# A two-layer image tower on one core: token search in three parts, chosen experts in the same stage, and a reordered first attention

## Chip, cores and metric

One core of one Trainium2 chip runs the whole program. The metric is the device time in microseconds (us) of that core. Of the kernel before, three runs are shown: 2080.99, 2083.64 and 2084.97, median 2083.64 us.

## What is computed

64 images of 3x224x224 are cut into 196 patches each, so there are 12544 tokens of width 128. Two layers follow:

```python
h = L0_tok(x)                                  # patches @ w + b
h = h + L0_attn(layernorm(h))                  # quantized q, k, v; causal attention inside one image
h = h + L0_ffn(layernorm(h))                   # each of 8 experts picks its own 1024 tokens
h = h + L1_attn(layernorm(h))                  # 8 heads
h = h + L1_ffn(layernorm(h))                   # each token picks 2 of 8 experts
# inside L0_ffn
logits = x_flat @ Wr                           # [12544, 8]
probs = softmax(logits, axis=0)                # over the tokens
vals, idx = top_k(probs.T, 1024)               # [8, 1024]
h = gelu(x_flat[idx] @ W1 + b1);  out_e = h @ W2 + b2
output = zeros.at[idx].add(vals[..., None] * out_e)
```

All 1024 tokens of an expert have to be found exactly, ties by the lowest token number. The change touches the first attention and the first expert layer (`L0_attn`, `L0_ffn`).

## The kernel before

The program has four stages, one behind the other, each with its own instruction streams for the five engines and with semaphores between them: `embed_and_attend`, `topk_experts`, `attend_and_route`, `routed_experts`. Between stages all engines meet.

**First attention, `embed_and_attend`.** The work is cut into 32 units of two images (4 tiles of 98 tokens). The engines run one software pipeline: in iteration n an engine does, for instance, the patch matmuls of unit n, the first norm and quantization of unit n-1, scores of unit n-2, mixing and projection of unit n-3 and the routing logits of unit n-4. The order inside an iteration is written out by hand for each engine, and an engine runs it strictly in order.

- SP (`emit_sp`, L380): in iteration n it first loads the images of unit n (12 DMAs, L270 and L271) once the pixels of unit n-2 have been copied out of the same half of the two-deep `img`, then it waits for the second norm of unit n-5 (L391) and stores `xn2` and `h2`, then the logits of unit n-6. The 12 loads of the next unit stand behind that wait in the queue.
- PE (L421): turn `hT` (L427), patches 0 and 1, turn `xd`, patch 2, the query-key matmul, turn `xn2` (L449), patch 3, turn `probs`, scores, patch 4, mix, patch 5, projection, patches 6 and 7, logits.
- ACT (L523): copies of `hcur`, `xdT`, `uT`; one copy of four pixel columns into `pix` (L539); `xn2T`, `probsT`, `mixT`; four exponentials (L559); `hT` with the bias (L566); the logits.
- DVE (L580): first norm and quantization of unit n-1 (L587 to L605), two row maxima for each image of unit n-2 (L614), and for unit n-3 the residual `h2`, its statistics and, after a wait for POOL's root (L636), the second norm `xn2` (L641).
- POOL (L647): the root for the first norm of unit n-1, two pixel columns (L664), the root for the second norm of unit n-3, two more pixel columns.

**Choice of tokens, first inner block of `topk_experts`.** The 8x12544 logits are read back as [128, 784]: 16 partitions for each expert. After maximum and exponential, a bisection (`settle`, L851) fixes the 30 bits of each expert's threshold probability from the top, one bit for each of 30 steps: DVE counts the values at or above a candidate (L854), PE sums the counts of the 16 partitions (L801), DVE updates `cur` and `bit`. Then prefix counts are formed (two scans, L874 and L881), written to DRAM (L751), read back twice with one row for each block of 112 tokens (L755, L756), and turned into a table `rise`. For each expert `past` marks the blocks that each of 1024 slots lies behind (L893), PE looks up the right block row by a matmul (L818), and DVE counts inside the block (L899). In all 16 groups of 512 slots are looked up, and then two instructions write all token numbers (L903, L904). POOL makes the constants of later stages meanwhile (`made.make`, `groups.constants`, L781).

**Chosen experts, second inner block (L940).** 16 groups of 512 tokens, two for each expert. POOL gathers the rows of a group with four indirect DMAs (L965) into a two-deep `xg`, PE turns them, computes the logit again for the weight, and the two layers (L1013, L998), ACT does the GELU (L1056) and the weighting (L1072), DVE adds the bias (L1112), and POOL adds the rows to `h` in DRAM with four indirect DMAs (L977). In its stream a gather of group n-1 and a scatter of group n-5 alternate. Before the scatter of every new expert POOL waits until the earlier scatters have landed (L972 to L974), since experts can share a token.

Of the kernel before, what the change touches and what calls it, by code (L numbers as in the profile page):

```python
# [15 lines left out]
D = 128  # L16
# [181 lines left out]
def embed_and_attend(nc, sb, ps, sem, early, x, w_tok, b_tok, wq, wk, wv, wr, hd_dram, ident, ident_b, ones,  # L198
                     mask_qk, halfpow, logits_dram, xn_dram):
    with ExitStack() as ph:  # L200
# [178 lines left out]
        def emit_sp(sp):  # L379
            def emit(n, k):  # L380

                if live(n, 0, UNITS) and not (isinstance(n, int) and n == 0):
                    wait(sp, pix_ready, n - 1, apart=True)
                    wait(sp, pix_ready_pool, 2 * (n - 1))
                    load_images(sp, n, k)
# [17 lines left out]
        def emit_pe(pe):  # L403
            def patch(n, k, js):
                if not live(n, 0, UNITS):
                    return
                if 0 in js:
                    wait(pe, pix_ready, n + 1)
                    wait(pe, hT_ready, n)
                if half // 2 in js:  # L410
                    wait(pe, pix_ready_pool, 2 * n + 2)
# [9 lines left out]
            def emit(n, k):  # L421
# [17 lines left out]
                if live(n, 2, UNITS):  # L439
# [4 lines left out]
                              start=True, stop=True).then_inc(u_ready, 1)  # L444
                if live(n, 4, UNITS):
# [5 lines left out]
                patch(n, k, [3])  # L451
# [70 lines left out]
        def emit_act(act):  # L522
            def emit(ahead, k_ahead):  # L523
# [6 lines left out]
                if live(n, 2, UNITS):  # L530
                    u = n - 2
                    wait(act, xd_turned, u + 1)
                    act.copy(xdT[:, (k - 2) % 2, :], p_tr[:, 0:COLS]).then_inc(xdT_ready, 1)
                    wait(act, u_ready, u + 1)
# [5 lines left out]
                if live(n, 4, UNITS):  # L540
                    u = n - 4
                    wait(act, xn2_turned, u + 1)
                    act.copy(xn2T[:, (k - 4) % 2, :], p_tr[:, 0:COLS]).then_inc(xn2T_ready, 1)
                if live(n, 3, UNITS):
                    u = n - 3
                    wait(act, probs_turned, u + 1)
                    for m in range(2):
                        act.copy(probsT[:, (k - 3) % 2, m, :], p_ptr[m][:, 0:CAUSAL]).then_inc(probsT_ready, 1)
                    wait(act, mixed, u + 1)
                    act.copy(mixT[:, (k - 3) % 2, :], p_mm[:, 0:COLS]).then_inc(mixT_ready, 1)  # L550
                if live(n, 2, UNITS):
                    u = n - 2
                    wait(act, max_ready, (u + 1) * 2)
                    if not isinstance(u, int) or u >= 4:
                        wait(act, h2_step, (u - 3) * H2_STEPS)
                    for m in range(2):
                        for i in range(2):
                            c = slice(0, TILE) if i == 0 else slice(TILE, CAUSAL)
                            act.activation(probs[:, (k - 2) % 2, m, c], p_score[m][:, c], ACT.Exp,  # L559
                                           bias=negmax[:, (k - 2) % 2, m, i:i + 1],  # L560
                                           accum_out=rowsum[:, (k - 2) % 4, 2 * m + i:2 * m + i + 1]
                                           ).then_inc(exp_ready, 1)
                if live(n, 0, UNITS):
# [3 lines left out]
                                   bias=bias[:, 0:1]).then_inc(hT_ready, 1)  # L567
                if live(n, 4, UNITS):
# [10 lines left out]
        def emit_dve(dve):  # L579
            def emit(n, k):  # L580
                if live(n, 1, UNITS):
# [10 lines left out]
                    st.then(dve.tensor_tensor(cent[:], hcur[:, r], bcast(mv[:, s, :, 0], D), ALU.subtract))  # L592
# [14 lines left out]
                    assert st.k == LN_STEPS, st.k  # L607
                if live(n, 2, UNITS):
# [8 lines left out]
                if live(n, 3, UNITS):  # L617
# [18 lines left out]
                    wait(dve, rstd2_ready, 2 * (u + 1))  # L636
                    if not isinstance(u, int) or u >= 2:
                        wait(dve, xn2_stored[s], (u // 2) * 16 if isinstance(u, int) else (u - s) * 8)
# [1719 lines left out]
```

## Time and profile before

| | |
|---|---|
| median of three runs | 2083.64 us |
| the profiled execution's own time | 2064.71 us |
| its span, first to last instruction | 2063.0 us |
| mean granted TensorE clock | 0.915 |
| PE, DVE, POOL, ACT busy, share of the span | 82, 60, 55, 51% |
| first attention | 0 to 518 us |
| choice of tokens | 518 to 655 us |
| chosen experts | 655 to 872 us |
| second attention and routed experts | 872 to 2063 us |

Busy time is execution on the engine; register, wait and DMA-issuing instructions do not count, except that POOL's indirect DMAs appear as busy, since POOL makes their descriptors. Every stage has its own limit, so the shares over the whole span say little; the rows further down are read stage by stage. In the rows "idle before" is the time in which the engine stood still ahead of an instruction, and the name behind the arrow is what ended it; "issue" means that the profile shows no releaser.

### The profile page before, as it was taken

Reading aid. Unit: us, or ns where it says so; the run is one execution under the profiler, and the core shown is the slowest. Engines: PE = TensorE matmul, PEld = TensorE weight load, DVE = VectorE, ACT = ScalarE, POOL = GpSimd, SP = SyncE. Lnnn points to the kernel's source line nnn. Section 1 sums busy time; section 2 is a strip of 40 time slices with the busy share of each in tenths; the row PEclk is TensorE's granted clock in tenths of the full one; section 3 lists DMA queues with packets and bytes.
Section 4 is the critical chain, followed back from the end, with each engine's and each line's share of the span. In section 5 each row is a group of like instructions: output and inputs, shape, how many; then the busy total and the mean of one; then the engine's idle time right before and its main releaser. Section 6 shows DMA issues by size and latency. Waiting matters only on the chain. (4 is left out here: it accounts for less than half of the span.)

```text
span 2063.0 us, 44563 instructions
## 1 busy us (share of the span) xinstructions
PE 1694.0 (82%) x13061; PEld 1251.6 (61%) x13062; DVE 1242.6 (60%) x4881; ACT 1048.1 (51%) x2435; POOL 1135.7 (55%) x1035
## 2 busy tenths in 40 slices
PE   4888988886223978469999999999995699999996
PEld 2555555554111655336767666666774589898985
DVE  2788888884564100068999999999987222222321
ACT  2555565553000654247676666666662355555553
POOL 2343443441302788612566666666666487877876
PEclk8999999997555998769999999999997799999998
DMA  8877878861001333321111111111111477776774
GB/s 204 192 193 193 203 189 202 194 145 36 8 8 53 63 66 64 34 75 33 42 51 50 51 51 50 52 50 52 45 41 48 116 135 138 127 135 120 137 132 80
DMA packets 271692, 199.05 MB, mean 96 GB/s; under 512 B 26121, under 2 KB 251947, under 8 KB 271531
## 3 DMA queue, kind: packets, MB, share of 16 engines
q1 hardware_dynamic: 221547, 161.65, 31.2%
q0 software_dynamic: 49984, 35.38, 12.6%
q8 instruction: 86, 1.41, 0.3%
q14 instruction: 75, 0.61, 0.1%
HBM read 144.12 MB, written 52.80 MB: 95 GB/s over the span
## 5 line engine op out<-in xcount | busy, mean ns | idle before, releaser
L2227 POOL DMA_INDIRECT out_dram<-r_yw,r_idx x212 | 328.4, 1549 | 116.8 <-issue 63.3
L2099 POOL DMA_INDIRECT rows_scratch<-routed_row,slot_u x256 | 251.4, 982 | 205.2 <-DVE slot_u L2050 141.9
L2295 ACT ACTIVATE r_hT<-r_p_up,r_b1T 128x256 f32<-128x256 f32 x424 | 192.7, 474 | 113.8 <-PE r_p_up L2269 109.3
L1773 ACT ACTIVATE a_probsT<-a_p_sc 98x392 f32<-98x392 f32 x384 | 170.5, 498 | 154.5 <-PE a_p_sc L1554 90.5
L2256 PEld LDWEIGHTS r_p_y<-w_all,r_hT 128*128 128x128 f32 x1696 | 224.1, 193 | 11.2
L2256 PE MATMUL r_p_y<-w_all,r_hT 128*128 x1696 | 224.6, 276 | 0.0
L2269 PE MATMUL r_p_up<-r_xgT,r_w1e 128*128 128x256 f32 x848 | 222.3, 386 | 0.6 <-ACT r_xgT L2300 0.6
L413 PE MATMUL p_embed<-pix,w_pix 96*128 96x392 f32 x512 | 208.4, 514 | 4.8 <-ACT pix L539 4.8
L656 POOL TENSOR_SCALAR vare<-mv 98x4 f32<-98x4 f32 x64 | 30.5, 477 | 281.3 <-DVE mv L634 205.4
L2312 DVE TENSOR_TENSOR r_yb<-r_p_y,b_all 128x256 f32<-128x256 f32 x106 | 45.0, 425 | 191.4 <-PE r_p_y L2256 182.1
L1870 DVE TENSOR_REDUCE a_negmax<-a_p_max 98x2 bf16<-98x392 f32 x256 | 131.8, 555 | 41.1 <-PE a_p_max L1521 40.9
L2269 PEld LDWEIGHTS r_p_up<-r_xgT,r_w1e 128*128 128x128 f32 x848 | 147.4, 194 | 12.8 <-DMA r_w1e<-in_L_ffn_W_dram 1.0
L965 POOL DMA_INDIRECT xg<-xn_scratch,take x64 | 62.0, 969 | 139.0 <-DVE take L1093 116.6
L1543 PE MATMUL a_p_sc<-q_var,kT 64*98 64x392 f32 x512 | 116.4, 531 | 1.7 <-ACT a_probsT L1773 1.7
L977 POOL DMA_INDIRECT h_scratch<-yw,give x64 | 100.7, 1573 | 25.9 <-issue 23.4
L664 POOL COPY pix<-img 96x784 f32<-96x784 f32 x64 | 96.4, 1509 | 31.1 <-DMA img<-in_x_dram 31.1
L413 PEld LDWEIGHTS p_embed<-pix,w_pix 96*128 96x128 f32 x512 | 86.1, 196 | 30.7 <-ACT pix L539 5.1
L1582 PE MATMUL a_p_q<-wqkvT,a_xnT 128*98 128x384 f32 x256 | 100.8, 519 | 3.5 <-ACT q_var L1814 2.8
L539 ACT COPY pix<-img 96x1568 f32<-96x1568 f32 x32 | 92.4, 2889 | 19.5 <-DMA img<-in_x_dram 19.4
L641 DVE TENSOR_SCALAR xn<-h,mv,rstd 98x128 f32<-98x128 f32 x128 | 66.5, 579 | 49.5 <-issue 46.4
L1814 ACT ACTIVATE q_var<-a_p_q,gains_var 128x392 f32<-128x392 f32 x128 | 76.4, 677 | 36.3 <-PE a_p_q L1476 36.3
L998 PEld LDWEIGHTS p_y<-w2e,ffn_hT 128*128 128x128 f32 x512 | 70.8, 205 | 38.5 <-issue 37.8
(354 smaller groups left out, 4004.3 us busy)
## 6 DMA issues: line engine op xcount, KB each, us to landing
img<-in_x_dram SPq DMA_DIRECT2D x192, 196.0 KB, 4.2
img<-in_x_dram SPq DMA_DIRECT2D x192, 189.0 KB, 4.4
r_w1e<-in_L_ffn_W_dram SPq DMA_DIRECT2D x106, 256.0 KB
r_xg<-rows_scratch SPq DMA_DIRECT2D x106, 130.0 KB
xn_scratch<-xn SPq DMA_DIRECT2D x32, 196.0 KB
h_scratch<-h SPq DMA_DIRECT2D x32, 196.0 KB
h<-h_scratch SPq DMA_DIRECT2D x32, 196.0 KB
h3b<-h_scratch SPq DMA_DIRECT2D x32, 196.0 KB
```

What stands on the lines that cost most here:

```text
L413: last = pe.matmul(p_embed[:, 0:COLS], w_pix[:, j, :], pix[:, k % 2, j, :], start=(j == 0), stop=(j == half - 1))
L664: pool.tensor_copy(pix[:, k_ahead % 2, js, :], by_column(k_ahead, js)).then_inc(pix_ready_pool, 1)
L977: pool.indirect_dma_start(hd_dram, bass.IndirectOffsetOnAxis(ap=give[:, (k - 5) % 4, t:t + 1], axis=0), yw[:, (k - 5) % 2, t, :], None, co ...
L1543: pe.matmul(p_sc[p][:, 0:2 * PAIR], kT[rows, s4, o:o + TILE], q_var[rows, s4, var:var + 2, o:o + PAIR], start=True, stop=False, skip_group ...
L1582: pe.matmul(p_q[t % 2][0:TILE, 0:3 * D], xnT[:, u % 2, t * TILE:(t + 1) * TILE], wqkvT[:], start=True, stop=True).then_inc(qkv, 1)
L1773: act.activation(probsT[:, u % 2, i, :], p_sc[i % 2][:, 0:2 * PAIR], ACT.Exp).then_inc(exped, 1)
L1870: dve.tensor_reduce(negmax[:, u % 2, group + 1, h], src.rearrange("p (h c) -> p h c", h=2), X, ALU.max, negate=True).then_inc(maxed, 1)
L2099: pool.indirect_dma_start(rows_dram, bass.IndirectOffsetOnAxis(ap=slot_u[:, u % ROWS, c, t:t + 1], axis=0), row[:, u % ROWS, c, t, :], Non ...
L2227: pool.indirect_dma_start(acc_dram, bass.IndirectOffsetOnAxis(ap=idx[:, (k - 3) % 4, t:t + 1], axis=0), yw[:, (k - 3) % 4, t, :], None, co ...
L2256: last = pe.matmul(p_y[k % 2][:, t, :], hT[:, (k - 2) % 2, f, t * 128:(t + 1) * 128], w2e[:, bass.ds(e, 1), f, :], start=(f == 0), stop=(f ...
L2269: pe.matmul(p_up[f][:, 0:G], w1e[:, (k - 1) % 4, f * 128:(f + 1) * 128], xgT[:, (k - 1) % 2, :], start=True, stop=True).then_inc(up, 1)
L2295: act.activation(hT[:, (k - 1) % 2, f, :], p_up[f][:, 0:G], ACT.Silu, bias=b1T[:, bass.ds(e * FC + f, 1)]).then_inc(act_h, 1)
```

## The change

**First attention.** The second norm moves from the end of DVE's iteration into the next iteration, behind the subtraction of the mean of the first norm. POOL computes both roots first and then copies its four pixel columns in two copies back to back. ACT copies its four pixel columns in two halves and the exponentials of the first image come before `hT`, those of the second behind it. PE does patch 3 ahead of the turn of `xn2`.

**Choice of tokens.** The probability's 32 bits are cut into a high and a low half; 9 steps narrow the high half and 11 the low half, each to a third: DVE counts at one candidate, ACT at another with Sign, PE sums both. Constants for later stages are made by POOL after the exponential, so beside the search. The prefix counts are laid out as records of one block each and moved to their place by 8 DMAs inside on-chip memory. Token numbers are written for each group as it is looked up.

**One stage.** Both inner blocks become one. Gathers go into a ring of 8 groups, the first six before any scatter; the look-ups of experts 3 to 7 are placed among PE's expert work; two experts' weights are loaded at the start of the stage. The copies `take`, `give` and `wre` fall away.

```diff
@@ emit_pe
+                patch(n, k, [3])
                 if live(n, 4, UNITS):
                     u = n - 4
                     wait(pe, h2_step, (u + 1) * H2_STEPS)
                     for t in range(TPU):
                         last = turn(p_tr[:, t * TILE:(t + 1) * TILE], xn2[:, (k - 4) % 2, t, :])
                     last.then_inc(xn2_turned, 1)
-                patch(n, k, [3])
@@ emit_act
+            def pixels(n, k, first, end):
+                if not live(n, 0, UNITS):
+                    return
+                if first == 0:
+                    image_there(act, n, k)
+                act.copy(pix[:, k % 2, first:end, :], by_column(k, slice(first, end))).then_inc(pix_ready, 1)
...
-                if live(ahead, 0, UNITS):
-                    image_there(act, ahead, k_ahead)
-                    js = slice(0, half // 2)
-                    act.copy(pix[:, k_ahead % 2, js, :], by_column(k_ahead, js)).then_inc(pix_ready, 1)
...
+                pixels(ahead, k_ahead, 0, 2)
...
+                pixels(ahead, k_ahead, 2, 4)
...
+                exps(n, k, 0)
                 if live(n, 0, UNITS):
                     wait(act, embedded, n + 1)
                     wait(act, h_turned, n - 1)
                     act.activation(hT[:, k % 2, :], p_embed[:, 0:COLS], ACT.Identity,
                                    bias=bias[:, 0:1]).then_inc(hT_ready, 1)
+                exps(n, k, 1)
@@ emit_dve
-                    st.then(dve.tensor_tensor(cent[:], hcur[:, r], bcast(mv[:, s, :, 0], D), ALU.subtract))
+                    st.mark(dve.tensor_tensor(cent[:], hcur[:, r], bcast(mv[:, s, :, 0], D), ALU.subtract))
+                    second_norm(n, k)
+                    wait(dve, ln_step, st.base + st.k)
@@ emit_pool
-                        (1, ln_step, 8, mv, vare, rstd, rstd_ready, LN_STEPS),
-                        (3, h2_step, 13, mv2, vare2, rstd2, rstd2_ready, H2_STEPS))):
+                        (4, h2_step, 13, mv2, vare2, rstd2, rstd2_ready, H2_STEPS),
+                        (1, ln_step, 8, mv, vare, rstd, rstd_ready, LN_STEPS)):
...
+                if live(ahead, 0, UNITS):
+                    image_there(pool, ahead, k_ahead)
+                    for part in range(2):
                         js = slice(half // 2 + 2 * part, half // 2 + 2 * part + 2)
                         pool.tensor_copy(pix[:, k_ahead % 2, js, :], by_column(k_ahead, js)).then_inc(pix_ready_pool, 1)
@@ topk_experts, search: DVE, then ACT
-                    def settle(i, at, values):
...
+                for i, step in enumerate(STEPS):
+                    dve.wait_ge(cand_ready, i + 1)
+                    now = cand[:, place(i)]
+                    dve.tensor_scalar(junk[:], keys(i), now[:, 0:1], None, ALU.is_ge, ALU.add, accum_out=cnt[:, 0:1]
+                                      ).then_inc(tallied, 1)
...
+                    dve.tensor_scalar(signed[:], sign[:], step, None, ALU.mult).then_inc(narrowed, 1)
+                    dve.scalar_tensor_tensor(nxt[:], spread[:], ahead, now, ALU.mult, ALU.add).then_inc(narrowed, 1)
...
+                    dve.wait_ge(summed, i + 1)
+                    dve.tensor_scalar(enough[:], p_up[i % 2][:, 0:2], 0.0, None, ALU.is_ge, ALU.add,
+                                      accum_out=passed[:]).then_inc(narrowed, 1)
+                    dve.wait_ge(narrowed, 3 * (i + 1) + (i > len(HIGH) - 1))
+                    ins = dve.scalar_tensor_tensor(cand[:, 3 if turning else place(i + 1)], signed[:], passed[:], nxt[:],
+                                                   ALU.mult, ALU.add)
...
+                    dve.scalar_tensor_tensor(key[:], high[:], cand[:, 3, 1:2], low[:], ALU.add, ALU.add
+                                             ).then_inc(cand_ready, 1)
...
+                for i in range(len(STEPS)):
+                    act.wait_ge(cand_ready, i + 1)
+                    act.activation(junk_act[:], keys(i), ACT.Sign, bias=cand[:, place(i), 1:2],
+                                   accum_out=cnt[:, 1:2]).then_inc(tallied, 1)
@@ prefix counts and look-up
-                    sp.dma_start(g_dram.rearrange("(p b) k -> p (b k)", p=128), scan[:]).then_inc(g_out, 16)
...
+                sp.wait_ge(v, V_RECS)
+                for e in range(EXPERTS):
+                    sp.dma_start(block_rec_b[:, e, 0:BLK + 2], rec_b[PER * e:PER * (e + 1)]
+                                 ).then_inc(recs_in if e else lg_in, 16)
...
+                        dve.wait_ge(hit, 4 * (i + 1))
+                        dve.tensor_tensor(tok_u[:, 4 * i:4 * i + 4], tokf[:, 4 * i:4 * i + 4], p_g[i % 2][:, :, BLK],
+                                          ALU.add).then_inc(tok_ready, 1)
@@ POOL, gathers and scatters
+                def gather(n, first=0, end=GT):
+                    wait(pool, turned, n - RINGX + 1)
+                    pool.wait_ge(tok_ready, n + 1)
...
+                for n in range(AHEAD):
+                    gather(n)
+                half = GT // 2
+                between = {1: [(6, 0, GT), (7, 0, GT)], 3: [(8, 0, GT), (9, 0, GT)], 5: [(10, 0, GT), (11, 0, GT)],
+                           7: [(12, 0, GT), (13, 0, half)], 9: [(13, half, GT), (14, 0, GT)], 11: [(15, 0, GT)]}
+                for u in range(GROUPS):
+                    scatter(u)
+                    for n, first, end in between.get(u, ()):
+                        gather(n, first, end)
@@ PE, look-ups among the expert work
+                for e in range(3):
+                    look(e)
+                places = {(0, FC): 3, (1, 2): 4, (1, FC): 5, (2, 2): 6, (2, FC): 7}
```

## Rows read from the trace of the kernel before

**Rows 1.** The page, busy time of each engine over the whole span

```profile
PE 1694.0 (82%) x13061; PEld 1251.6 (61%) x13062; DVE 1242.6 (60%) x4881; ACT 1048.1 (51%) x2435; POOL 1135.7 (55%) x1035
```

**Rows 2.** Busy time by stretch: PE, PEld, DVE, ACT, POOL, clock, DMA share, GB/s

```profile
533.00:605.00 72.00, 17.59 (x60) 15.04 (x60) 46.99 (x177) 0.00 (x0) 4.83 (x15) 0.50 0.00 0
655.00:866.00 211.00, 157.87 (x832) 113.38 (x832) 17.54 (x73) 95.37 (x169) 162.51 (x128) 0.86 0.37 63
200.00:400.00 200.00, 178.44 (x926) 109.53 (x924) 164.86 (x605) 116.88 (x257) 83.47 (x84) 1.00 0.82 196
```

**Rows 3.** Stretch 200 to 400 us: line L566, and two waits (total, times, longest)

```profile
L566 ACT ACTIVATE hT<-p_embed,bias x14: 597/599/601, 200.8 to 386.1; 128x392 f32<-128x392 f32 x14
...
  PE p_htr L419: 12.0, 14
...
DVE xn L641 <- issue: 21.5, 14, 1.5
```

**Rows 4.** Groups of instructions, 200 to 400 us: busy, mean ns, idle before

```profile
L641 DVE TENSOR_SCALAR xn<-h,mv,rstd 98x128 f32<-98x128 f32 x56 | 31.2, 616 | 21.5 <-issue 21.5
L595 DVE TENSOR_TENSOR amax<-amax,rstd 98x4 f32<-98x4 f32 x14 | 19.4, 1385 | 8.3 <-POOL rstd L658 8.3
L600 DVE TENSOR_SCALAR rounded<-cent,qscale 98x128 f32<-98x128 f32 x56 | 12.2, 282 | 0.5
...
L664 POOL COPY pix<-img 96x784 f32<-96x784 f32 x28 | 42.2, 1508 | 0.0
```

**Rows 5.** Timeline: SP's store, last image load, ACT's pixel copy; issue to landing

```profile
291.20 0.32 SPq L392 DMA_DIRECT2D xn_scratch<-xn  x1
...
300.28 0.61 SPq L271 DMA_DIRECT2D img<-in_x_dram  x1
...
305.56 2.89 ACT L539 COPY pix<-img 96x1568 f32<-96x1568 f32 x1
...
img<-in_x_dram SPq DMA_DIRECT2D x192, 196.0 KB, 4.2
```

**Rows 6.** Timeline of the choice of tokens: its start, and one late step

```profile
517.94 0.35 SPq L749 DMA_DIRECT2D lgt<-logits_scratch  x1
...
522.70 5.13 DVE L835 COPY row<-row 1x128 f32<-1x128 f32 x1
...
524.23 3.52 POOL L1181 MEMSET vals<- 98x4096 f32 x1
...
529.25 0.95 ACT L825 ACTIVATE prob<-lgt,col 128x784 f32<-128x784 f32 x1 [13.23 <-DVE col L839]
...
530.11 0.19 ACT L825 ACTIVATION_READ_ACCUMULATOR prob<-lgt,col 128x1 f32 x1
...
602.06 0.58 PE L801 MATMUL p_s<-cnt,same_expert 128*128 128x1 f32 x2 [1.78 <-DVE junk L854]
```

**Rows 7.** Timeline from the last scan to the first gather, and the eight marks

```profile
613.08 1.79 DVE L881 TENSOR_TENSOR_SCAN scan<-one_run,gt 128x784 f32<-128x784 f32 x1
...
616.65 0.34 SPq L751 DMA_DIRECT2D prefix_scratch<-scan  x1
...
629.46 1.09 DVE L891 TENSOR_TENSOR rise<-table,prev 112x896 bf16<-112x896 f32 x1 [12.83 <-DMA prev<-prefix_scratch]
...
L893 DVE TENSOR_SCALAR past<-slots,prev 112x1024 bf16<-112x1024 f32 x8 | 5.4, 747 | 0.0
...
655.19 1.26 POOL L965 DMA_INDIRECT xg<-xn_scratch,take  x1 [116.64 <-DVE take L1093]
```

**Rows 8.** Chosen experts: POOL's two groups, first scatter, one late scatter

```profile
L977 POOL DMA_INDIRECT h_scratch<-yw,give x64 | 100.7, 1573 | 25.9 <-issue 23.4 <-ACT yw L1072 2.5
L965 POOL DMA_INDIRECT xg<-xn_scratch,take x64 | 62.0, 969 | 139.0 <-DVE take L1093 116.6 <-issue 18.6 <-PE p_x L1023 3.8
...
685.67 1.65 POOL L977 DMA_INDIRECT h_scratch<-yw,give  x1 [2.25 <-ACT yw L1072]
...
851.61 1.55 POOL L977 DMA_INDIRECT h_scratch<-yw,give  x1 [2.56 <-issue]
```

More of the change, by code:

```diff
@@ L382, in emit @@
                 if live(n, 0, UNITS) and not (isinstance(n, int) and n == 0):
-                    wait(sp, pix_ready, n - 1, apart=True)
+                    wait(sp, pix_ready, 2 * (n - 1), apart=True)
                     wait(sp, pix_ready_pool, 2 * (n - 1))
@@ L522, in emit_act, with exps @@
         def emit_act(act):
+            def pixels(n, k, first, end):
[4 more added lines that the diff above has]
+                act.copy(pix[:, k % 2, first:end, :], by_column(k, slice(first, end))).then_inc(pix_ready, 1)
+            def exps(n, k, m):
+                if not live(n, 2, UNITS):
+                    return
+                u = n - 2
+                wait(act, max_ready, 2 * u + m + 1)
+                if m == 0 and u >= 4:
+                    wait(act, h2_step, (u - 3) * H2_STEPS)
+                for i in range(2):
+                    c = slice(0, TILE) if i == 0 else slice(TILE, CAUSAL)
+                    act.activation(probs[:, (k - 2) % 2, m, c], p_score[m][:, c], ACT.Exp,
+                                   bias=negmax[:, (k - 2) % 2, m, i:i + 1],
+                                   accum_out=rowsum[:, (k - 2) % 4, 2 * m + i:2 * m + i + 1]).then_inc(exp_ready, 1)
             def emit(ahead, k_ahead):
@@ L548, in emit @@
                         act.copy(probsT[:, (k - 3) % 2, m, :], p_ptr[m][:, 0:CAUSAL]).then_inc(probsT_ready, 1)
+                if live(n, 4, UNITS):
+                    u = n - 4
+                    wait(act, xn2_turned, u + 1)
+                    act.copy(xn2T[:, (k - 4) % 2, :], p_tr[:, 0:COLS]).then_inc(xn2T_ready, 1)
+                pixels(ahead, k_ahead, 2, 4)
+                if live(n, 3, UNITS):
+                    u = n - 3
                     wait(act, mixed, u + 1)
                     act.copy(mixT[:, (k - 3) % 2, :], p_mm[:, 0:COLS]).then_inc(mixT_ready, 1)
[L551 to L562, printed above, removed]
+                exps(n, k, 0)
                 if live(n, 0, UNITS):
@@ L579, in emit_dve, with second_norm @@
         def emit_dve(dve):
+            def second_norm(n, k):
+                if not live(n, 4, UNITS):
+                    return
+                u = n - 4
+                s = (k - 4) % 2
+                wait(dve, rstd2_ready, 2 * (u + 1))
+                if u >= 2:
+                    wait(dve, xn2_stored[s], (u // 2) * 16)
+                    wait(dve, xn2_turned, u - 1)
+                for t in range(TPU):
+                    dve.tensor_scalar(xn2[:, s, t, :], h2[:, s, t, :], mv2[:, s, t, 0:1],
+                                      rstd2[:, s, t:t + 1], ALU.subtract, ALU.mult).then_inc(h2_step, 1)
             def emit(n, k):
@@ L607, in emit @@
                     assert st.k == LN_STEPS, st.k
+                else:
+                    second_norm(n, k)
                 if live(n, 2, UNITS):
@@ L635, in emit @@
                     dve.wait_ge(h2_step, st.base + st.k)
-                    wait(dve, rstd2_ready, 2 * (u + 1))
-                    if not isinstance(u, int) or u >= 2:
-                        wait(dve, xn2_stored[s], (u // 2) * 16 if isinstance(u, int) else (u - s) * 8)
-                        wait(dve, xn2_turned, u - 1)
-                    for t in range(TPU):
-                        st.mark(dve.tensor_scalar(xn2[:, s, t, :], h2[:, s, t, :], mv2[:, s, t, 0:1],
-                                                  rstd2[:, s, t:t + 1], ALU.subtract, ALU.mult))
-                    assert st.k == H2_STEPS, st.k
+                    assert st.k == H2_STEPS - TPU, st.k
             straight(dve, emit, DEPTH, UNITS)
@@ L648, in emit @@
                 n, k = ahead - 1, k_ahead - 1
-                for part, (skew, step, at, m, v, r, ready, per) in enumerate((
-                        (1, ln_step, 8, mv, vare, rstd, rstd_ready, LN_STEPS),
-                        (3, h2_step, 13, mv2, vare2, rstd2, rstd2_ready, H2_STEPS))):
+                for skew, step, at, m, v, r, ready, per in (
+                        (4, h2_step, 13, mv2, vare2, rstd2, rstd2_ready, H2_STEPS),
+                        (1, ln_step, 8, mv, vare, rstd, rstd_ready, LN_STEPS)):
                     if live(n, skew, UNITS):
@@ L696, in topk_experts @@
     BLOCKS = ALL // BLK
+    BPP = RUN // BLK
     ST = CAP // 128
     NT = EXPERTS * ST
[L699 to L895 removed]
```

759 lines of the change are left out of this document (372 added, 387 removed).

## The prediction, on record before the changed kernel was seen

> **What bounds the kernel now.** I read the page first. PE is the busiest engine, but no engine is near full over the span [rows 1], so I cut it into stages and read the busy time of each stretch. In the steady first attention PE is busy for 178.4 of 200 us and DVE for 164.9. In the search of 72 us PE has 17.6 us of work, DVE 47.0, ACT none: a chain of small steps, bound by nothing but its length. In the chosen experts POOL is busy for 162.5 of 211 us [rows 2].
>
> First attention: 14 `hT` lie between 200.8 and 386.1 us, so a unit takes 185.3/13 = 14.25 us [rows 3]. PE works 0.892 of that, 12.7 us, and waits 1.5; its wait for `hT` alone is 12.0/14 = 0.86 us [rows 2, 3]. DVE has 0.824 x 14.25 = 11.7 us of work, and two waits for POOL's roots: 21.5/14 = 1.53 us ahead of `xn`, 8.3/14 = 0.59 ahead of `amax` [rows 3, 4]. Together 13.9: DVE's own chain closes the period and PE waits for it. Part of its work is no work: `xn` takes 616 ns for what `rounded` does in 282, so 4 x 0.33 = 1.3 us a unit, and an `amax` of four columns takes 1.39 us, some 1.2 too long [rows 4]. Both stand beside POOL's pixel copies.
>
> Choice of tokens: from the logits' load at 517.94 to the first gather at 655.19, 137.3 us [rows 6, 7]. Chosen experts: POOL spends 1.57 us on a scatter and 0.97 on a gather, and 0.30 between two (18.6/61 for gathers) [rows 8]. 64 x 1.87 + 64 x 1.27 = 201 of the 211 us. Neither PE nor ACT sets that stage, POOL's list of 128 DMAs does.
>
> **First attention, part by part.** The wait ahead of `xn` goes (the root is made while DVE begins the next unit), and so does the one ahead of `amax`, which now has `second_norm`, 4 x 0.28 us, and a reduction in front. That takes 2.1 us from DVE's chain: 14.25 - 2.1 = 12.1 us. Then PE is next, 12.7 us. ACT has the same work, 0.584 x 14.25 = 8.3 us, and its copy of 2.89 us in two halves [rows 2, 5] hides as before. `hT` waits for two exponentials where it waited for four, so PE's 0.86 us wait should go. What is late next: PE turns `xn2` one patch later, but `xn2` is made after `hcur`, the statistics and the subtraction, so it comes at about the same point as before; I leave 0.4 us of waiting there and 0.2 for the mixing. That makes 13.3 us.
>
> SP's queue gives the same number. The 12 image loads stand behind the store of `xn2`. Store at 291.20, last load issued at 300.28, 4.2 us from issue to landing, so images there at about 304.4; ACT copies them at 305.56 [rows 5]. Moving `xn2` leaves the store at the same point of the unit, so the images need 304.4 - 291.2 = 13.2 us of a period, and at 13.3 they come just in time. 0.95 us on some 28 steady units (70 to 470 us) is **-27 us**. Bounds: PE's floor, 1.5 x 28 = -43; nothing gained, 0, or a loss if POOL's two copies, now back to back, hold `xn2`.
>
> On this the Trainium skill has a rule (SBUF — State Buffer, section SBUF: two separate sides): DVE in a two-port mode or with two inputs, and GpSimd, share one port pair as an exclusive lock, and the loser waits for the whole instruction. The trace agrees with it where `xn` and `amax` stretch [rows 4], and by the rule alone the two copies in a row could take the gain back; by the rows the sum counts the same 2.5 us of stretching as before.
>
> **Start of the search.** Now 517.94 to 533: 15.1 us. The copy L835 takes 5.13 us beside POOL's memsets, 3.52 us of them `vals` [rows 6]; for one row 0.2 is usual. These memsets move behind the exponential: -4.9. The sums' reciprocal leaves the path and one conversion of 784 columns (1.0) comes: -1.8. **-6.7 us**, 8.4 stay.
>
> **The search.** A step now is 72.0/30 = 2.40 us [rows 2]. The new step: ACT's pass, 529.25 to 530.30 with the accumulator read, 1.05 us (DVE's count at the same time is no longer); then PE, as now from 602.06, 0.59; then `enough` with its read, 0.24, the last update 0.16, and four hand-overs of 0.04: 2.2 us [rows 6]. `signed` and `nxt` lie under PE's turn. One PE offset matmul more a step falls into PE's idle time. 20 x 2.2 + 1.3 for the join of both halves = 45.3. POOL now makes its constants beside it; where one of its long instructions holds a small DVE operation, that shows: I take 4 us, between 0 and the 5.1 that L835 shows plus as much again, 10. 72.0 - 49.3 = **-22.7 us**. Bounds of the step are 2.05 (no hand-overs) and 2.4 (as now): -3 and +4 us.
>
> **From threshold to first gather.** Now 605 to 655.19, 50.2 us. The way through DRAM, 616.65 to 629.46, is 12.8 of it, the eight `past` marks stand ahead of any count (8 x 0.67), and 16 groups are counted before the first gather [rows 7]. New: equals 1.1, scan 1.8 [rows 7], one column operation 0.2, ties 1.1, scan 1.8, tail 0.2, PE's two matmuls 1.2, record columns 0.7: 8.1 us. Eight DMAs on SP, 0.43 us apart, the last landing 2.4 us on, and 0.6 for small packets: 6.0 (bounds 5 and 12.8, what DRAM takes now). Marks of expert 1 0.75, PE's look-up 0.6, four counts and their sum 1.3, and 0.7 to the first gather: 17.4 us in all, so **-32.8 us**. The other 15 groups take 1.7 us each on DVE where POOL needs 5.1 for a group's gathers; they hide. Sum of the three parts: -62.2 us, 75 in place of 137.
>
> **Chosen experts.** POOL's list stays 201 us, and no merging shortens it. Now the first scatter comes 685.67 - 655.19 = 30.5 us after the first gather, and 10 us of waits are spread over the stage, 2.56 ahead of a late scatter while the one before lands [rows 8]. New: six groups of gathers take 6 x 5.08 = 30.5 us. PE's chain to the first scatter starts as now, but has five look-ups in it, about 1 us each at the lower clock, and DVE counts groups 14 and 15 (2.7 us) ahead of the first bias: 30.5 + 5 + 2.7 = 38.2, so POOL waits 7.7. Behind it 16 x 7.49 + 10 x 5.08 = 170.6, one landing wait 2.2, one wait for group 13, 1.3: 212 in place of 211. **0 us**, bounds -8 (no wait for the first scatter) and +10. Six groups ahead cost nothing and bring nothing, as POOL issues as many DMAs. If that wait were gone the landing waits would be next.
>
> **Sum.** -27 - 6.7 - 22.7 - 32.8 + 0 = -89 us against the profiled execution of 2064.7: 1975.5. That execution ran 18.9 us below the median of the runs; by the median, which is what I forecast, 2083.6 - 89 = **1994 us**. Second attention and routed experts are untouched.
>
> **Rivals.** *PE's floor*: both waits of the attention vanish and POOL's constants hide: -43 - 66 = -109, 1975. For it, PE's work and DVE's 12.1; against it, the images' 13.2 us. Chance 0.18.
>
> *The lock moves*: POOL's two copies, 2 x 1.5 us, run when `xn2`, `amax` and `deq` are due. The period stays 14.25 and only -62 is left: 2022. For it: 2.5 us of stretching exist already with one copy at a time [rows 4]. Chance 0.19.
>
> *POOL starves at the start of the experts*: gathers run beside DVE's marks (0.75 us each, seven of them) and counts, and PE's look-ups delay the first scatter beyond 38 us: +10 to +12, so 2005. Beside this rival stands a page of the Trainium skill (SBUF — State Buffer, the box on DVE blocking SWDGE): POOL cannot write descriptors while DVE holds the pair. No row of before has both at once. Chance 0.12.
>
> *Slower than before, one mechanism*: `xn2` behind both copies and the root, so 3.8 us later in the unit, and with it the store and the 12 image loads behind it on SP. The images' 13.2 us then grow to 17.0. It decides where the period passes 14.25 + 62/28 = 16.5 us: then +70 - 62 = +8, 2092. Against it: DVE reaches `xn2` 1.8 us after the statistics, about when POOL finishes the root, so it is mostly ahead of the copies. Chance 0.04. *The change does not do what it says* (ACT's Sign pass much longer than its Exp pass, so two engines give no shorter step and 20 steps of 3.6 us take the 72 back): 2017, chance 0.02, in the range.
>
> **How the numbers follow.** The forecast's case, 1994, holds 0.45; its own range is 1980 to 2008. The range over the cases goes from the PE floor with a little more, 1965, to the moved lock with slow DMAs, 2026; some 0.13 is left out. All cases but one are faster. A measurement of this kernel tells 0.2%, 4 us, from no change; faster by more than that 0.94, within it 0.02, slower 0.04.
>
> **What the profile would show.** Right: `hT` every 13.3 us; DVE without the wait ahead of `xn`; steps of 2.2 us, 20 of them, ACT and DVE ending together; first gather 75 us after the logits' load; first scatter 38 us after the first gather, and the stage POOL-bound, near 212 us. Wrong: a period near 14.3 or above with `xn2` stretched or PE waiting for it; ACT waiting for images; steps over 2.4 us; a first gather beyond 80 us; gathers above 1.1 us beside the look-ups; or a stage of experts far from 212 us, which would mean that POOL's list isn't what bounds it.

## The result, and the profile after

The changed kernel takes 2006.2 us (median of 2003.38 to 2009.72) against 2082.55 for the one before on the same chip: ratio 0.9633, 95% interval 0.9614 to 0.9653, so 76 us less. The forecast was 1994 with a range of 1965 to 2026. The profiled execution is the one of 2003.38 us, its span 2001.7.

The page after, busy time of each engine over the whole span:

```profile
PE 1703.6 (85%) x13083; PEld 1263.3 (63%) x13084; DVE 1224.1 (61%) x4791; ACT 1071.5 (54%) x2510; POOL 1138.6 (57%) x1037
```

Against [rows 1] the busy times have hardly moved. Busy time by stretch, columns as in [rows 2]: the search, the chosen experts, the steady first attention.

```profile
494.00:543.00 49.00, 22.73 (x84) 20.55 (x83) 38.11 (x145) 21.05 (x41) 17.18 (x34) 0.50 0.00 0
559.00:790.00 231.00, 167.34 (x888) 120.47 (x888) 35.54 (x169) 95.39 (x169) 161.42 (x128) 0.82 0.32 52
200.00:400.00 200.00, 193.02 (x1009) 120.46 (x1008) 179.54 (x665) 128.64 (x293) 91.51 (x93) 1.00 0.91 214
```

The search of 72 us is 49 long now, with ACT at work in it. The experts have grown from 211 to 231 us although POOL is busy for as long as before (161 and 162.5). In the attention PE, DVE and the DMA engines (0.82 to 0.91) all do more in the same 200 us.

First attention, columns of the groups as in [rows 4], and the two longest waits on a DMA (total us, times, longest):

```profile
L579 ACT ACTIVATE hT<-p_embed,bias x16: 587/587/588, 200.6 to 396.2; 128x392 f32<-128x392 f32 x16
```

```profile
L629 DVE TENSOR_SCALAR rounded<-cent,qscale 98x128 f32<-98x128 f32 x60 | 28.1, 529 | 0.5
L604 DVE TENSOR_SCALAR xn<-h,mv,rstd 98x128 f32<-98x128 f32 x60 | 16.6, 340 | 0.0
L625 DVE TENSOR_SCALAR deq<-amax 98x4 f32<-98x4 f32 x15 | 11.4, 758 | 0.5
L627 DVE TENSOR_TENSOR qscale<-qscale,rstd 98x4 f32<-98x4 f32 x15 | 10.3, 688 | 0.5
L624 DVE TENSOR_TENSOR amax<-amax,rstd 98x4 f32<-98x4 f32 x15 | 6.4, 429 | 0.5
L688 POOL COPY pix<-img 96x784 f32<-96x784 f32 x30 | 44.8, 1521 | 10.4 <-DMA img<-in_x_dram 10.4
```

```profile
ACT pix L530 <- DMA img<-in_x_dram: 14.8, 13, 1.7
POOL pix L688 <- DMA img<-in_x_dram: 10.4, 12, 1.3
```

16 `hT` from 200.6 to 396.2 are 195.6/15 = 13.04 us a unit, 14.25 before [rows 3]. DVE's two waits for POOL's roots are gone. The stretching beside POOL's copies has moved from `xn` (616 ns, now 340) and `amax` (1385, now 429) to `rounded` (282, now 529), `deq` and `qscale` (170 and 162 before, now 758 and 688); it is still about 2.6 us a unit, and ACT and POOL now wait for images.

The choice of tokens, timeline: the load, the row copy that took 5.13 us in [rows 6], the first two steps with the longest of POOL's memsets (one of 1.08 us stands just ahead of it), the end of the search, the marks of experts 0 and 1, the first gather, the first scatter.

```profile
486.16 0.35 SPq L826 DMA_DIRECT2D lgt<-logits_scratch  x1
...
490.98 0.21 DVE L1064 COPY row<-row 1x128 f32<-1x128 f32 x1
...
494.25 1.03 DVE L1076 TENSOR_SCALAR_CACHE_REDUCE junk<-prob_high,cand 128x784 bf16<-128x784 f32 x1
...
496.43 1.03 DVE L1076 TENSOR_SCALAR_CACHE_REDUCE junk<-prob_high,cand 128x784 bf16<-128x784 f32 x1
...
497.38 4.74 DVE L1080 TENSOR_SCALAR signed_step<-cand_sign 128x2 f32<-128x2 f32 x1
...
498.58 3.51 POOL L1225 MEMSET vals<- 98x4096 f32 x1
...
542.77 1.03 DVE L1105 TENSOR_SCALAR_CACHE_REDUCE eq<-prob_key,cand 128x784 f32<-128x784 f32 x1
...
550.87 5.13 SPq L831 DMA_DIRECT2D block_rec<-rec  x8
553.00 0.75 DVE L1132 TENSOR_SCALAR past<-slots,block_rec 112x1024 bf16<-112x1024 f32 x1 [2.16 <-DMA block_rec<-rec]
...
557.49 0.75 DVE L1132 TENSOR_SCALAR past<-slots,block_rec 112x1024 bf16<-112x1024 f32 x1 [3.74 <-DMA block_rec<-rec]
...
559.76 1.26 POOL L842 DMA_INDIRECT xg<-xn_scratch,tok_u  x1 [47.02 <-DVE tok_u L1146]
...
612.61 1.64 POOL L852 DMA_INDIRECT h_scratch<-yw,tok_u  x1 [22.68 <-ACT yw L1020]
```

Load to first count 8.1 us, search 48.5, threshold to first gather 17.0: 73.6 us in place of 137.3 [rows 6, 7]. A step takes 2.18 us; the second took 3.9 longer. The first scatter comes 52.9 us after the first gather, 30.5 before [rows 8].

### The profile page after: what moved, and what is told of

Same layout as the page of the kernel before. It is cut to its first block and busy times, and to the rows that moved or that the text cites. A ratio compares the mean times of both kernels' runs of the same rounds, so it can differ in the third digit from the quotient of the medians.

```text
span 2001.7 us, 44426 instructions
## 1 busy us (share of the span) xinstructions
PE 1703.6 (85%) x13083; PEld 1263.3 (63%) x13084; DVE 1224.1 (61%) x4791; ACT 1071.5 (54%) x2510; POOL 1138.6 (57%) x1037
## 5 line engine op out<-in xcount | busy, mean ns | idle before, releaser
L680 POOL TENSOR_SCALAR vare<-mv 98x4 f32<-98x4 f32 x64 | 30.4, 476 | 229.5 <-DVE mv L665 195.4
L2313 PEld LDWEIGHTS r_p_up<-r_xgT,r_w1e 128*128 128x128 f32 x848 | 146.9, 193 | 12.6 <-DMA r_w1e<-in_L_ffn_W_dram 1.0
L852 POOL DMA_INDIRECT h_scratch<-yw,tok_u x64 | 100.3, 1567 | 49.6 <-ACT yw L1020 29.0
L530 ACT COPY pix<-img 96x784 f32<-96x784 f32 x64 | 98.3, 1542 | 45.7 <-DMA img<-in_x_dram 45.5
L1157 DVE TENSOR_TENSOR yb<-p_y,b2e 128x512 f32<-128x512 f32 x16 | 11.1, 691 | 150.4 <-PE p_y L976 131.4
L842 POOL DMA_INDIRECT xg<-xn_scratch,tok_u x64 | 61.5, 961 | 66.2 <-DVE tok_u L1146 47.0
L1553 PEld LDWEIGHTS a_p_max<-kT,q_var 64*98 64x98 bf16 x1024 | 52.3, 123 | 69.5 <-issue 35.8
```

The costliest lines, as they stand in the source:

```text
L530: act.copy(pix[:, k % 2, first:end, :], by_column(k, slice(first, end))).then_inc(pix_ready, 1)
L852: pool.indirect_dma_start(hd_dram, bass.IndirectOffsetOnAxis(ap=tok_u[:, u * GT + t:u * GT + t + 1], axis=0), yw[:, u % RINGY, t, :], None ...
L2313: pe.matmul(p_up[f][:, 0:G], w1e[:, (k - 1) % 4, f * 128:(f + 1) * 128], xgT[:, (k - 1) % 2, :], start=True, stop=True).then_inc(up, 1)
```

## The experiments

Below, "choice" runs from the logits' load to the first gather, "stage" from the first gather to the start of the last scatter, "rest" from there to the end. Ratios are to the kernel before on the same chip; the one to compare is 0.9633.

**1. Both kernels once more, and each half of the change alone.** The first question was 15 us: forecast 38 us to the first scatter, measured 52.9. These rows of the timeline of after, in order of time, show where they go:

```profile
573.33 0.33 DVE L1143 TENSOR_SCALAR_CACHE_REDUCE hits<-p_g,slot 128x112 bf16<-128x112 f32 x1 [0.83 <-remote]
574.30 1.06 PE L948 MATMUL p_x<-ident,xg 128*128 128x128 f32 x4
576.20 2.08 PE L966 MATMUL p_up<-xgT,w1e 128*128 128x512 f32 x2 [0.84 <-issue]
588.09 0.59 ACT L1040 COPY xgT<-p_x 128x512 f32<-128x512 f32 x1 [7.72 <-remote]
588.73 1.87 PE L957 MATMUL p_l<-wr_all,xgT 128*128 128x1 f32 x8 [10.45 <-issue]
593.81 0.34 DVE L1143 TENSOR_SCALAR_CACHE_REDUCE hits<-p_g,slot 128x112 bf16<-128x112 f32 x1 [18.41 <-remote]
```

TensorE is given the transposition of group 1 at 574.30, and it should be done at 575.4. ScalarE, which waits for nothing else, copies it at 588.09. "remote" means that no instruction ended at the time of the release. The trace also keeps when each semaphore was raised: the one of this transposition went up at 588.07, 12.7 us after the modelled end of its last instruction, and the product behind it (modelled end 578.3) at 592.26. I call such a result late; when it was given and when its semaphore was raised are recorded, but its end is modelled, so whether TensorE worked late or only reported late isn't told apart.

> The kernel before, unchanged, profiled once more beside the others of this set. Two theories of the 15 us by which the first scatter came later than forecast (52.9 us after the first gather, forecast 38). Between 573 and 592 us of the profile after, TensorE issued a transposition at 574.9 that was only turned over to ScalarE at 588.07. Theory A, the new stage does it (its look-ups or its run of gathers hold TensorE): this profile looks like the one before, first scatter 30.5 us after the first gather, second half (from the end of the experts to the end) 1197 us, span near 2063. Theory B, TensorE is slowed from time to time in any kernel and the profiled execution of before (18.9 us below its median) was a lucky one: this profile has a span near 2080, with the extra 15 to 20 us as late TensorE results somewhere in it, and the second half nearer 1211 us.

> The kernel after, unchanged, profiled a second time. Theory A: first scatter again 53 us after the first gather, with the same idle time of about 12 us on TensorE in the first 30 us of the experts. Theory B: the late results stand elsewhere or are gone, the first scatter comes about 38 to 41 us after the first gather, and the stage takes 212 to 220 us in place of 231.

> The first attention of before with the new choice of tokens and experts. By the parts of the two profiles (137.3 to 73.6 us for the choice, 211.0 to 230.6 for the experts) this gives -44 us, 2038. By my forecast's terms -62, 2021. If the new attention's 32 us are not independent of the rest (images and second norm now reach the search later or earlier), the result lies off 2006 + 32 = 2038.

> The new first attention with the old choice and experts. By the two profiles -32 us, 2051 (a unit takes 13.04 us in place of 14.25). If the two parts add up, this one and the other sum to -76 us.

For the third the edit is the whole diff without the hunks of the first attention, for the fourth those hunks alone.

| us | choice | first scatter | stage | rest | time, ratio |
|---|---|---|---|---|---|
| before, first profile | 137.3 | +30.5 | 209.4 | 1198.4 | 2064.7 |
| before again | 137.1 | +35.3 | 214.2 | 1216.3 | 2086.9 |
| after, first profile | 73.6 | +52.9 | 229.0 | 1212.9 | 2003.4 |
| after again | 73.5 | +52.6 | 228.2 | 1221.7 | 2009.1 |
| choice only | 71.5 | +53.4 | 230.3 | 1221.6 | 0.9798 (0.9781 to 0.9816) |
| attention only | 137.1 | +35.3 | 214.1 | 1218.7 | 0.985 (0.9834 to 0.9867) |

Both theories hold a part. The kernel before has late results too: none in its first profile, up to 5.0 us here, and more in the second attention, most of them about 1 us late. The 22 us between its two profiled executions lie where they are (4.8 in the stage, 17.9 in the rest); that they are the cause in the rest is read from the place, and no run removes them there. The rest is the same code in all rows and took 1213 to 1222 us wherever late results occur, so the first profile of before was the exception. But the late first scatter is the change's own: +52.6 to +53.4 three times, against +35.3 twice. The halves are worth 2.0% and 1.5%, 42 and 31 us, and add up to the 76 within the noise.

**2. What GpSimd issues, and in which order.**

> Four groups of gathers ahead (16 in a row at the start, then always 4 gathers and 4 scatters in turn) in place of six (24 in a row, then 8 and 8). Theory B2: TensorE's results come late while GpSimd issues a long run of gathers, and are there again some 3 us after the last of the run. The last gather of the first run then comes 10 us earlier, the first scatter about 43 us after the first gather in place of 53, the short runs later in the stage hold TensorE by under 1 us each, and the stage takes about 216 us in place of 229: 10 to 14 us less than the kernel after (ratio to before 0.9798 less 0.018, some 0.955). Theory C, the order of TensorE's list (look-ups between the products) makes the first scatter late, whatever GpSimd does: no change, 0 to +3 us.

```diff
-    AHEAD = 6
+    AHEAD = 4
...
+                between = {u: [(u + 4, 0, GT)] for u in range(GROUPS - 4)}
```

> Six groups ahead as in the kernel after, but a group's first-run gathers wait until the group two before it is turned by TensorE, so that the first run of 24 is broken where TensorE is behind. Theory B2: after 12 gathers the run pauses until TensorE has turned group 1, at about 575; first scatter 40 to 46 us after the first gather, stage 218 to 224, 6 to 12 us less than the kernel after. Theory C: the first scatter stays at 53 or comes later.

```diff
                 for n in range(AHEAD):
+                    wait(pool, turned, n - 1)
                     gather(n)
```

Four ahead: 2013.5 us, 0.9636 (0.9609 to 0.9662), no change. The first scatter came at +43.5 as expected, yet the stage is 229.3: what isn't gathered ahead is gathered later by the same queue. What counts is the time in which GpSimd has nothing to issue, and that is 23 us with both. My sum for this run had left that out. After-turn: 2005.9 us, 0.9604 (0.9578 to 0.9629), which can't be told from the kernel after; stage 224.9, just short of the 218 to 224 expected. Its first run stopped after 12 gathers, and no result of that run was over 4.1 us late, as theory B2 has it. But the first scatter came at +48.7 and not at 40 to 46, since it stood behind group 5's gathers, which waited for TensorE until +43.7.

**3. No gathers at all in the first 30 us.**

> The first six groups' rows are loaded by 24 plain DMAs on SP (128 consecutive rows each, as many bytes as a gather) in place of GpSimd's gathers, so the rows given to the products are not the chosen ones; GpSimd issues nothing until the first scatter. Theory B2 (GpSimd's run of gathers makes TensorE's results late): in the first 30 us of the experts no result is over 0.5 us late, TensorE's clock rises within 15 us of its first product, and the first scatter comes 35 to 40 us after the first load. Theory F (TensorE is held by the 24 landings themselves, or by the look-ups at the low clock): its results are late here too, and the first scatter comes at 48 us or later. GpSimd has 30 us less to issue, so the stage takes some 190 us or less, which says nothing.

```diff
+                for n in range(AHEAD):
+                    sp.wait_ge(tok_ready, n + 1)
+                    for t in range(GT):
+                        r = (n * GT + t) * 128
+                        sp.dma_start(xg[:, n, t, :], xn_dram[r:r + 128]).then_inc(g_in[5 + n // 2], 16)
...
-                for n in range(AHEAD):
-                    gather(n)
```

This kernel leaves out the choice of rows for the first six groups, so it serves for its trace alone. No result is over 0.3 us late in the first 58 us, and then they begin, with GpSimd's first run of eight gathers (48.6 to 57.5 us after the first load). So it is not an execution free of late results, as the first of before was. The same transposition in this kernel (its lines stand 5 or 6 further down), and its first scatter; the first load was at 554.64:

```profile
567.01 0.60 PE L954 MATMUL p_x<-ident,xg 128*128 128x128 f32 x4
567.79 0.58 ACT L1046 COPY xgT<-p_x 128x512 f32<-128x512 f32 x1
...
586.77 1.84 POOL L857 DMA_INDIRECT h_scratch<-yw,tok_u  x1 [76.68 <-ACT yw L1026]
```

First scatter at +32.1 with all look-ups in TensorE's list. Two stretches of 32 us from the first gather or load on, of after and of this kernel:

```profile
560.00:592.00 32.00, 15.30 (x61) 9.55 (x60) 10.95 (x63) 3.83 (x5) 22.93 (x24) 0.50 0.18 50
```

```profile
555.00:587.00 32.00, 24.95 (x152) 16.99 (x150) 22.24 (x141) 13.08 (x20) 0.23 (x1) 0.82 0.18 51
```

The DMA engines move as much in both (50 and 51 GB/s). With the gathers TensorE gets 61 matmuls off and stays at 1.2 GHz until 600 us, 40 us after the first gather; without, 152, and it is at 2.4 GHz from 11.7 us on. The clock alone is not the cause: the first profile of before was at 1.2 GHz until 17.2 us after its first gather with nothing late, and after the kernel after has reached 2.4 GHz it still has results 5.5 us late beside its next gathers. So it is neither the bytes that land nor the look-ups, but GpSimd's own gathers in a run. In every row with late results they come back some 3 to 5 us after the run's last gather is issued:

| kernel | gathers in the first run, last at | latest result | all back at | first scatter | idle before it | stage |
|---|---|---|---|---|---|---|
| before, first profile | 16, +19.5 | none late | | +30.5 | 5.2 | 209.4 |
| before again | 16, +19.5 | 5.0 us | +22.9 | +35.3 | 10.0 | 214.2 |
| four ahead | 16, +19.3 | 7.2 | +22.9 | +43.5 | 23.3 | 229.3 |
| after | 24, +29.2 | 14.0 | +34.1 | +52.9 | 22.5 | 229.0 |
| after again | 24, +29.4 | 12.5 | +34.2 | +52.6 | 22.2 | 228.2 |
| after-turn | 12, +14.2 | 4.1 | +17.3 | +48.7 | 18.4 | 224.9 |
| no gathers | 0 | none late | | +32.1 | | |
| broken run (below) | 12, +14.2 | 3.0 | +17.2 | +43.0 | 0 | 222.5 |

The other five profiles of this set that start with 24 gathers in a row (choice only, and those of parts 4 and 5 but the broken run) have all back at +34.1 to +34.3, and attention only, with 16, at +22.8. "Idle before it" is the first scatter's place less about 5.06 us for each group gathered ahead of it (and less 17.7 for constants in the last row). Stage less idle is 204 to 207 us in the first six rows: all but some 2 us of the stage's difference is GpSimd's wait for the first scatter.

**4. Look-ups earlier, constants later, images first.**

> The last five look-ups stand earlier in TensorE's list (all before the second group's products end), so that VectorE has counted all slots before it adds the first bias. In the run with four groups ahead VectorE counted groups 14 and 15 for 3 us after the first lower product was done. If that wait is what is left of the 53 us: first scatter 49 to 50, stage -3 us, total -3 us against the kernel after. If the look-ups now wait for VectorE's marks (0.75 us and eight counts for each expert) in front of the first products: no gain or +3.

```diff
-                places = {(0, FC): 3, (1, 2): 4, (1, FC): 5, (2, 2): 6, (2, FC): 7}
+                places = {(0, 1): 3, (0, FC): 4, (1, 0): 5, (1, 1): 6, (1, 2): 7}
```

2007.3 us, 0.9641 (0.9622 to 0.966): no gain. The first scatter came at +55.1, the look-ups' results are among the late ones, and more of them now stand ahead of the products.

> GpSimd's constants for the second attention are made after the first six groups' gathers, where it waits 23 us for the first scatter, and no longer beside the search. If the one long step (4.74 us between two updates at 497.4, beside a memset of 3.5 us) is the two engines' shared port, it goes: -4 us against the kernel after, search 20 steps of 2.18. If the memsets then hold the counts of the later slots or the first bias, the stage of the experts gives it back. If the long step has another cause, no change.

```diff
-                made.make(pool)
-                groups.constants(pool)
                 for n in range(AHEAD):
                     gather(n)
+                made.make(pool)
+                groups.constants(pool)
```

The choice fell to 69.8 us and `next_cand`, 4.67 us at worst before, took 152 to 156 ns in all 20 steps; GpSimd's idle time ahead of the first scatter fell from 22.3 to 5.6 and the scatter stayed at +53.1. So the long step was GpSimd's memsets, at 3.7 us. The price depends on where they fall: in four other profiles (choice only, after-turn, no gathers, look-ups early) they held two steps for 1.3 and 2.2 us in place of one for 4.7, and the choice took some 2 us less than in the profiles of after. The time, 2007.1 us with 0.9624 (0.9595 to 0.9653), can't tell 3.7 us from nothing.

> In the first attention the 12 image loads of the next unit stand ahead of the stores of xn2 and h2 on SP in place of behind them. A unit takes 13.0 us in the kernel after, with 0.9 us of waiting for images by ScalarE and 0.7 by GpSimd. Theory D, the store's place in SP's queue sets the images' arrival (my forecast's 13.2 us): the waits on images go and a unit takes about 12.6 to 12.8 us, -6 to -12 us in all. Theory E, the 16 DMA engines (0.91 busy in that stretch) or TensorE (0.965 busy) set it: within 2 us of the kernel after.

```diff
-            def emit(n, k):
-                if live(n, 0, UNITS) and not (isinstance(n, int) and n == 0):
-                    wait(sp, pix_ready, 2 * (n - 1), apart=True)
-                    wait(sp, pix_ready_pool, 2 * (n - 1))
-                    load_images(sp, n, k)
+            def emit(ahead, k_ahead):
+                n, k = ahead - 1, k_ahead - 1
+                if live(ahead, 0, UNITS) and ahead > 0:
+                    wait(sp, pix_ready, 2 * (ahead - 1), apart=True)
+                    wait(sp, pix_ready_pool, 2 * (ahead - 1))
+                    load_images(sp, ahead, k_ahead)
```

1999.3 us, 0.9581 (0.9557 to 0.9605), so 11 us less than the kernel after by the ratios, and the logits' load at 471.1 in place of 484.0 (after again). 16 `hT` from 209.6 to 398.2 make 12.57 us a unit, no wait for images is left, and TensorE is what bounds it:

```profile
200.00:400.00 200.00, 196.49 (x1052) 126.27 (x1051) 183.12 (x685) 134.01 (x304) 94.67 (x96) 1.00 0.92 217
```

Theory D: the time inside its 6 to 12 us, the unit just under its 12.6. The DMA engines at 0.92 were no limit.

**5. Together.**

> Images first (-11 by its own run), constants later (-3.7 by its profile) and look-ups early together, with gathers six groups ahead as in the kernel after. If they add up: 18 us less than the kernel after, ratio to before 0.963 - 0.009 = 0.954, about 1991 beside a before of 2087. The constants now share GpSimd's wait for the first scatter with VectorE's last counts; if these collide, 3 us less of it.

1989.2 us, 0.9553 (0.9524 to 0.9582), as expected, though without help from the look-ups (first scatter +54.4, stage 229.5): images and search alone gave it.

> Images first, and GpSimd's first list broken where it held TensorE: the gathers of groups 0 to 2, then the constants of the second attention (17 us in the run with the constants later), then the gathers of groups 3 and 4, the first scatter, and group 5's gathers behind it. By theory B2 TensorE has its results from about 18 us after the first gather on, and the first scatter comes 42 to 45 us after the first gather with no idle GpSimd ahead of it: 201 us of DMAs, 17 of constants and 5 of landing waits make a stage of 223 us in place of 229, the search is 3.7 us shorter, and the images give 11: 20 us less than the kernel after, ratio to before about 0.9535. If the run of 12 gathers is enough to hold TensorE, or if the constants' memsets stretch VectorE's counts, the first scatter comes at 50 us or later and only the 15 us of images and search are left.

The hunk of the images, as above, and in GpSimd's list:

```diff
-                made.make(pool)
-                groups.constants(pool)
-                for n in range(AHEAD):
+                for n in range(5):
+                    if n == 3:
+                        made.make(pool)
+                        groups.constants(pool)
                     gather(n)
...
-                between = {1: [(6, 0, GT), (7, 0, GT)], 3: [(8, 0, GT), (9, 0, GT)], 5: [(10, 0, GT), (11, 0, GT)],
+                between = {0: [(5, 0, GT)], 1: [(6, 0, GT), (7, 0, GT)], 3: [(8, 0, GT), (9, 0, GT)], 5: [(10, 0, GT), (11, 0, GT)],
```

1987.3 us, 0.9506 (0.9489 to 0.9524), the lowest of all, though its interval just touches that of the run before it. GpSimd's list: last gather of group 2, the long memset, the last gather of group 4, the first scatter.

```profile
556.11 0.94 POOL L842 DMA_INDIRECT xg<-xn_scratch,tok_u  x1 [0.30 <-issue]
...
559.89 3.50 POOL L1225 MEMSET vals<- 98x4096 f32 x1
...
583.67 0.94 POOL L842 DMA_INDIRECT xg<-xn_scratch,tok_u  x1 [0.30 <-issue]
584.91 1.64 POOL L852 DMA_INDIRECT h_scratch<-yw,tok_u  x1 [0.30 <-issue]
```

Choice 69.6, first scatter +43.0 with no idle time ahead of it, stage 222.5 (expected 223), logits' load at 472.3. Against the profile of after again: 11.7 + 3.9 + 5.7 = 21.3 us, where 20 were forecast. It beats both kernels.

## Why the prediction held, and where it did not

**First attention, -27: measured -31.8** (-33.6 in the second pair, -31 by the times of that half alone). The mechanism is the one given: both waits of DVE gone, 2.5 us of stretching kept at other instructions (the lock of the Trainium skill, page SBUF — State Buffer, section SBUF: two separate sides, seen again where `rounded` takes 529 ns and `deq` 758 beside POOL's copies; it moved without making the sum worse), and the images just in time. The term that was mis-sized is the unit, 13.04 us for 13.3. That the store's place in SP's queue sets it, 13.2 us by the forecast, is shown by the run with the images first: 12.57, where TensorE's own work, 12.35 of it, is the floor that the first rival named as 12.7. (By the prediction's own rows 304.48 - 291.20 is 13.3; and in its rival of a slower kernel a unit of 17.0 us costs 2.75 x 28 = 77 us, not 70. Nothing rests on either.)

**Start -6.7, 8.4 left: 8.1. Search 49.3: 48.5**, steps of 2.18 for 2.2, and 3.9 us of POOL's constants for 4, shown by moving them (in four other profiles they fell so that they cost some 2 less). **Threshold to first gather 17.4: 17.0.** Together 75 forecast, 73.6 measured.

**Chosen experts, 0: measured +14** (214.2 to 228.2 between like executions; +19.6 between the two first profiles). The step that failed is "PE's chain to the first scatter starts as now, but has five look-ups in it, about 1 us each at the lower clock, and DVE counts groups 14 and 15 (2.7 us) ahead of the first bias: 30.5 + 5 + 2.7 = 38.2". Each term of it was fair or too high: without gathers the whole chain takes 32.1. What is missing is that TensorE's results are held while GpSimd issues its gathers in a run, and "six groups ahead cost nothing" is wrong for that reason: 24 in a row hold them until +34, 16 until +23. The profile of before could not show it, as in that one execution no result was late; the same kernel once more shows it.

The rival *POOL starves at the start of the experts* had the place and nearly the price (+10 to +12, 2005 in all; the time is 2006.2), but not the mechanism. GpSimd's gathers were not slowed beside DVE's marks: the first 24 took 940 to 1256 ns, mean 965, where the mean was 969 before [rows 8]. The box of the Trainium skill on DVE blocking SWDGE (page SBUF — State Buffer), which stood beside that rival, is therefore not what happened. The same page of the Trainium skill (section SBUF: two separate sides) says that a DMA cannot be slowed by a compute op, "and vice versa". The runs show TensorE held while GpSimd issues its DMAs, up to 14.0 us; whether that is by the ports isn't shown. In the second pair of profiles the attention gives -33.6, the choice -63.6, the experts +14.0 and the untouched rest +5.4 (it varied by 9 us between executions of this kernel): -77.8 where -89 was forecast, so 1994 became 2006.

**The median.** I set the sum against the profiled execution (2064.7) and carried it to the median, 19 us above, as a constant. That held, and for a reason I did not know: the second profile of before is 22 us longer, with late results that the first did not have. That the 19 us are the same thing is likely, and not shown.

## What to carry to other kernels

Ask of a run-ahead what the queue has to do while it waits: gathering further ahead gains only if the queue would be idle otherwise, and here the first scatter, not the number of groups ahead, set the idle time. Where a trace shows TensorE's results late beside a long run of GpSimd's indirect DMAs, break the run with other work of GpSimd's own; here that was worth 5.7 us of the stage. In a unit-pipelined loop look at what stands ahead of the next unit's loads in the DMA queue, before calling the DMA engines or the vector chain the bound.

## What the runs showed that I had not expected

While GpSimd issues 12 to 24 gathers back to back, results of TensorE are handed on up to 14 us after their instructions should have ended (17.4 in the run with everything together); ScalarE's and VectorE's are not (of 87 signals of ScalarE's and over 100 of VectorE's between 550 and 800 us of after again, none was over 0.25 us late; of TensorE's 118, 22 were over 0.5). Runs of 8 gathers later in the stage give 3 to 6 us in the kernel after, runs of 4 at most 1 in the kernel before. In the rest of the kernel before late results go with some 18 us. One profiled execution of before had none at all, so it depends on the chip or the execution. Why it happens, and whether an execution without a profiler has it as strongly, was not tried; nor were gathers with the same descriptors and fewer bytes, which would part the descriptors from the data.
